# First cross attention: the spread row maxima copied to SBUF by ScalarE before the shift reads them

## The reference, cut to what matters

```python
q = _ln((x @ Wq + bq).reshape(b, s1, H, HD), qn_w, qn_b)      # 16 heads of 32
kv = jnp.concatenate([y_main @ Wk + bk, y_main @ Wv + bv], axis=-1)
k = _ln(kv[..., :HD], kn_w, kn_b)
v = kv[..., HD:]
ctx = _attn(qT, k, v)            # softmax(q k^T * scale) v, over 1585 keys
ctx_dca = _attn(qT, k_dca, v_dca)  # the last 16 keys, their own softmax
ctx = ctx + DCA_WEIGHT * ctx_dca
```

## Time and profile before

| what | value |
|---|---|
| time, median of 3 runs | 2612.16 us (2611.98 to 2613.95) |
| the profiled execution's own time | 2601.18 us |
| its span | 2599.4 us |
| PE busy | 2277.8 us (88%) |
| DVE busy | 1655.2 us (64%) |
| ACT busy | 1182.7 us (46%) |
| POOL busy | 1042.8 us (40%) |
| mean granted clock of PE | 0.944 |

### The profile page before, as it was taken

The page is one execution under the profiler, slowest core; times in us unless marked ns, Lnnn a source line. Parts: engine busy times, 40 slices in busy tenths (PEclk is TensorE's granted clock), DMA queues, the critical chain, the costliest instruction groups (busy, mean ns, idle before and its releaser), DMA issues. The chain is left out here.

```text
span 2599.4 us, 45868 instructions
## 1 busy us (share of the span) xinstructions
PE 2277.8 (88%) x16206; PEld 1809.3 (70%) x16212; DVE 1655.2 (64%) x2676; ACT 1182.7 (46%) x2172; POOL 1042.8 (40%) x724
## 2 busy tenths in 40 slices
PE   4598899989987699987997899999999998788866
PEld 2576677767765488875776688888888876566644
DVE  3457787778787333334532388878888883676763
ACT  1345555555554133322312476766677662333242
POOL 3157788878887000000110154555455560100230
PEclk9689999999997799997998999999999998899979
DMA  3000000000000211202313100000000001211200
GB/s 109 1 26 26 27 2 27 27 27 2 27 2 2 80 53 63 65 21 67 79 35 107 33 18 18 27 26 10 19 26 26 1 1 65 63 37 44 78 0 17
DMA packets 104280, 89.91 MB, mean 35 GB/s; under 512 B 32753, under 2 KB 82433, under 8 KB 104081
## 3 DMA queue, kind: packets, MB, share of 16 engines
q1 hardware_dynamic: 103792, 87.28, 11.0%
q0 software_dynamic: 288, 0.00, 0.0%
HBM read 86.22 MB, written 1.05 MB: 34 GB/s over the span
## 5 line engine op out<-in xcount | busy, mean ns | idle before, releaser
L2249 POOL TENSOR_TENSOR xT<-xT,x1b_ring 128x512 f32<-128x512 f32 (+1 forms) x176 | 249.2, 1416 | 211.8 <-ACT x1b_ring L2379 205.6
L914 POOL TENSOR_TENSOR x0b_krstd<-x0b_krstd,minus_half 128x24 f32<-128x24 f32 x64 | 269.4, 4209 | 101.8 <-DVE x0b_krstd L984 78.0
L934 POOL TENSOR_TENSOR xT<-xT,x0b_ring 128x512 f32<-128x512 f32 (+1 forms) x176 | 252.1, 1432 | 82.4 <-ACT x0b_ring L1143 72.4
L111 DVE TENSOR_TENSOR x1b_plo<-x1b_ring,x1b_phi 128x512 fp32r<-128x512 f32 (+1 forms) x208 | 221.1, 1063 | 5.2 <-issue 4.9
L1143 ACT ACTIVATE x0b_ring<-x0b_ring 128x512 f32<-128x512 f32 (+1 forms) x208 | 130.9, 631 | 188.6 <-DVE x0b_ring L1012 182.3
L2394 ACT ACTIVATE x1b_ring<-x_ps,x1b_keymask 128x512 f32<-128x512 f32 (+1 forms) x208 | 143.1, 688 | 132.9 <-DVE xT L2321 126.9
L1036 DVE TENSOR_TENSOR x0b_ring<-x_ps,x0b_krstd 128x512 f32<-128x512 f32 (+1 forms) x208 | 142.6, 686 | 76.2 <-PE x_ps L819 74.8
L116 PE MATMUL x_ps<-x1b_qy,x1b_yT 128*128 128x512 f32 (+1 forms) x416 | 175.9, 423 | 4.3 <-ACT x1b_ring L2394 2.9
L2321 DVE SCALAR_TENSOR_TENSOR xT<-x_ps,x1b_keymask,xT 128x512 f32<-128x512 f32 (+1 forms) x176 | 131.2, 746 | 58.3 <-PE x_ps L118 57.4
L116 PE MATMUL x_ps<-x1b_phi,x1b_yv 128*128 128x512 f32 (+1 forms) x416 | 165.9, 399 | 1.5 <-ACT x1b_out_sb L2361 1.5
L118 PE MATMUL x_ps<-x1b_qy,x1b_yT 128*128 128x512 f32 (+1 forms) x416 | 164.3, 395 | 0.0
(11 more groups left out here) (587 smaller groups left out, 5748.1 us busy)
## 6 DMA issues: line engine op xcount, KB each, us to landing
x_y<-in_ctx_dram SPq DMA_DIRECT2D x8, 1536.0 KB
x_y<-in_ctx_dram SPq DMA_DIRECT2D x24, 512.0 KB, 3.8
a_wn<-in_L_attn_W_Q_dram SPq DMA_DIRECT2D x16, 256.0 KB, 3.1
a_wn<-in_L_attn_W_K_dram SPq DMA_DIRECT2D x16, 256.0 KB, 3.5
a_wn<-in_L_attn_W_V_dram SPq DMA_DIRECT2D x16, 256.0 KB, 4.2
a_won<-in_L_attn_W_O_dram SPq DMA_DIRECT2D x16, 256.0 KB, 2.8
x1a_wq<-in_L_xattn_Wq_dram SPq DMA_DIRECT2D x4, 1024.0 KB, 11.5
x1c_wo<-in_L_xattn_Wo_dram SPq DMA_DIRECT2D x8, 512.0 KB, 7.3
```

The costliest lines, as they stand in the source:

```text
L111: return v.tensor_tensor(lo, exact, hi.bitcast(F32), ALU.subtract)
L914: ins = g_.tensor_tensor(r, r, c.minus_half[:, 0:8].unsqueeze(1).broadcast_to([P, whole, 8]), ALU.pow)
L934: g_.tensor_tensor(total[half][0:m, :], old, src, ALU.add).then_inc(summed, 1)
L2249: g_.tensor_tensor(total[half][0:m, :], old, src, ALU.add).then_inc(summed, 1)
```

## The change

The spread maxima lose their own bank. PE writes them into the next bank of the rotation, which now has four banks (4 to 7), ACT copies the 128 x 512 block into SBUF (into `c.xn`, of which two tiles serve as `shift`, one for each half) and gives the bank back, and all 13 shifts of the half read that copy. PE no longer waits for `shifted` before it spreads; it waits for the rotation's bank. The preparation's small product moves from bank 4 to bank 3. Nothing is removed from any engine; ACT gets 16 copies.

```diff
+        shift = [c.xn[:, f, :] for f in range(2)]
...
-        S_BANKS, O_BANK, M_BANK, KV_BANKS = (0, 1, 2), 3, 4, (5, 6, 7)
+        S_BANKS, O_BANK, KV_BANKS = (0, 1, 2), 3, (4, 5, 6, 7)
...
-                for what, at in (("sums", 29), ("inverse", 30), ("maxima", 13)):
+                for what, at in (("spread", 15), ("sums", 29), ("inverse", 30), ("maxima", 13)):
...
                     f = half_at(part, n, 15)
                     if f is not None:
+                        bank, nth = place["spread", 2 * seq + f]
+                        pe.wait_ge(kv_free[bank], nth + 1)
                         pe.wait_ge(rowmax_done, 3 * (2 * seq + f) + 3)
-                        if not (part == "first" and f == 0):
-                            pe.wait_ge(shifted, TILES * seq + KT * f)
                         for t in range(4):
-                            mm = pe.transpose(ps[:, M_BANK, t * P:(t + 1) * P],
+                            mm = pe.transpose(ps[:, bank, t * P:(t + 1) * P],
                                               rowmax[:, f % 2, t:t + 1].broadcast_to([P, P]), c.ident[:, :])
                         mm.then_inc(max_spread, 1)
+                        pe.sem_inc(kv_full[bank], 1)
...
                         if t % KT == 0:
-                            v.wait_ge(max_spread, 2 * seq + t // KT + 1)
+                            v.wait_ge(shift_kept, 2 * seq + t // KT + 1)
                         v.wait_ge(kept, TILES * seq + (t + 1))
-                        v.tensor_tensor(slot, slot, ps[0:m, M_BANK, :], ALU.subtract).then_inc(shifted, 1)
+                        v.tensor_tensor(slot, slot, shift[(t // KT) % 2][0:m, :], ALU.subtract).then_inc(shifted, 1)
...
                 def step(part, seq, n):
+                    f = half_at(part, n, 15)
+                    if f is not None:
+
+                        bank = place["spread", 2 * seq + f][0]
+                        act.wait_ge(max_spread, 2 * seq + f + 1)
+                        if 2 * seq + f >= 2:
+                            act.wait_ge(shifted, KT * (2 * seq + f - 1))
+                        act.activation(shift[f % 2], ps[:, bank, :], ACT.Copy).then_inc(shift_kept, 1)
+                        act.wait_ge(shift_kept, 2 * seq + f + 1)
+                        act.sem_inc(kv_free[bank], 1)
                     f = half_at(part, n, 30)
```

More of the change, by code:

```diff
@@ L719, in x0_main_attention @@
         out_kept, normed, added = st.sem("out_kept"), st.sem("normed"), st.sem("added")
+        shift_kept = st.sem("shift_kept")
         apart = st.sem("apart")
@@ L802, in _ @@
                     for g in range(HG0):
-                        mm = pe.matmul(ps[:, M_BANK, 16 * t + 4 * g:16 * t + 4 * g + 4], qT[:, g, t * P:(t + 1) * P],
+                        mm = pe.matmul(ps[:, O_BANK, 16 * t + 4 * g:16 * t + 4 * g + 4], qT[:, g, t * P:(t + 1) * P],
                                        headkn[:, :], start=True, stop=True)
@@ L1124, in _ @@
                     for bp in range(2):
-                        src = ps[64 * bp:64 * bp + 64, M_BANK, 0:16 * T].rearrange("p (t k a) -> p t k a", t=T, a=2)
+                        src = ps[64 * bp:64 * bp + 64, O_BANK, 0:16 * T].rearrange("p (t k a) -> p t k a", t=T, a=2)
                         dst = qshift[64 * hp:64 * hp + 64, :].rearrange("p (t a k) -> p t a k", t=T, a=2)
```

## The result

The changed kernel takes 2645.66 us (median of 4 runs, 2644.87 to 2655.12) against 2613.05 us (4 runs, 2611.98 to 2618.49): 1.0142 times the time before, 95% interval 1.0112 to 1.0172. The medians differ by 32.6 us, the ratio and its interval make it 37 (29 to 45); +5 was forecast and +24 was the upper end of the range.

A forecast was written before the change was run, and what follows sets the result against it. PE was taken to bound the kernel. Delays at four places, 9.8 + 8.4 + 3.5 + 1.6 = 23.3 us, less 18.0 of bank waits gave +5.3, so 2617.5, rounded 2618 us; range 2600 to 2636.

The forecast's parts named there:

- A: Step 0 of each sequence: late DVE work delays POOL's power and the turned sums; +1.4 us, seven times, +9.8 us.
- B: Step 14: the shift meets a POOL add, so ACT's squares come late for PE; +1.2 us, seven times, +8.4 us.
- C: Step 24: the shift meets a POOL add and ends late, ACT and PE follow; +0.5 us, seven times, +3.5 us.
- the banks: PE's waits for rotation banks: a fourth bank can remove them all, a gain of 18.0 us.
- D: End of the stage: ten shifts against POOL's last adds, some eight falling between adds at +0.2 each; +1.6 us.
- The bound: Between 200 and 780 us PE sets the pace; a gain can come only from its 51.9 idle us.
- The removed waits: Four rows of PE's bank waits can go, 18.0 us, or 20.5 with the wait for `shifted`.
- second rival: Removed waits return as data waits and stretching falls into idle time; 2612 within 5 us, chance 0.16.
- The shift's length: Unchanged alone; beside POOL's adds the shift's mean goes from 683 to 900 to 1050 ns.
- The clock is no part of it: PE's granted clock, 0.98 between 200 and 780 us, was ruled out as a factor in what bounds the kernel.
- The signs: Expected in the profile: longer shifts and adds, bank waits nearly gone, POOL waits over 3 us, squares' waits 15 or more.
- DVE becomes the bound: Late stretches on DVE join up and use its idle time, so PE waits; 2627 to 2657 us, chance 0.16.

The follow-up runs named there:

- three_banks: Changed kernel, but the spread maxima keep a bank of their own and three banks rotate; 2659.16 us, 1.0191 times the kernel before.
- small_adds_after: Changed kernel with POOL's adds cut to 8 of 512 columns; 2565.67 us, 0.9847 times the kernel before.
- small_adds_before: Kernel before with POOL's adds cut to 8 of 512 columns; 2571.43 us, 0.987 times the kernel before.
- operand: Kernel before, but all 208 shifts read an SBUF tile (wrong numbers), without copies and with three banks; 2658.38 us, ratio 1.018.
- operand_last: Kernel before, but only the last sequence's 26 shifts read SBUF (wrong numbers); 2621.94 us against 2614.07, ratio 1.0031.

## Why the forecast had the sign and not the size

The forecast's terms add up to 3.7 us by the start of the eighth sequence (A, B and C less the banks) and 1.6 from there on (D). The traces have 19.2 and 15.0. So D, the last sequence and the end, is short by 13 us, and the sequences before it by 15: of their terms A was too small, B and C did not happen as described, and the banks were counted too high.

**The bound** (PE, its idle 52 us all there is to gain): right. Of PE's waits, though, "the rest are waits for data" named two rows and passed over two more, the maxima's 8.4 us and L111's 4.2, which both grew.

**The removed waits**: right as rows (18.0 to 1.3 us), too high as time: 18.0 us were taken off, three_banks against the change gives about 13. The 1.1 us that PE waited for Y11's bank (L761) came back fully (1.3 us a sequence), of the 0.9 us of K111's bank (L116) only 0.3, and the 0.5 us that came back at step 22 are lost again at step 23 to a longer wait for L111: a bank wait that goes is in part followed by the wait for data that it hid. The prediction knew that way out (its second rival) and gave it no value in the sum.

**The shift's length**: right: 1004 ns, inside 900 to 1050, single ones up to 1.79 us, alone the same as from PSUM (689 against 684 ns). The Trainium skill (SBUF — State Buffer, section on the two separate sides) describes a lock on a port pair shared by VectorE and GpSimd, held for a whole instruction. For POOL's adds the runs agree: 1004 ns beside adds, 689 without. For POOL's power they do not, and the measurement decides: 122 DVE instructions with two SBUF inputs lie inside a running power of the changed kernel and average 689 ns.

**The places.** What a middle sequence gains or loses, in us, averaged over five of them and counted from the first scores of one tile to those of another (the first scores of a tile stand in the step before its own). The columns are kernels less the kernel before; "short adds" is small_adds_after less small_adds_before; what stands there too is not the work of POOL's adds.

| tiles, and what lies there | forecast | change | operand | short adds |
|---|---|---|---|---|
| 0 to 1, W02's squares (C) | +0.5 | 0.0 | +1.2 | 0.0 |
| 1 to 3, maxima and T02 (A) | +1.4 | +2.4 | +1.2 | 0.0 |
| 3 to 6, the turned sums | 0 | +0.4 | +0.5 | +0.5 |
| 6 to 12, K111's bank, W11 | (bank) | +0.7 | +0.8 | 0.0 |
| 15 to 18, W13 (B) | +1.2 | +0.8 | +1.7 | +0.3 |
| 18 to 19, Y11's bank | (bank) | -1.3 | 0.0 | -1.3 |
| 20 to 25 | (bank) | +0.8 | +0.1 | 0.0 |
| sum | +0.5 | +3.8 | +5.4 | -0.4 |

The forecast's sum is 3.1 for A, B and C less 2.6 for all banks.

**A, step 0, taken as +1.4 us**: place and mechanism right, size low. In the fourth sequence the maxima's wait grows by 0.72 (1.21 to 1.93), T02 leaves PE 0.42 later behind products at half the clock, and the power is 0.5 us longer (4.68, 4.17 before). It begins 0.04 us behind the start of a shift of ordinary length. These make 1.6; the remaining 0.5 lies between T02 and the turned sums, where DVE is late. The waits of L847 stayed at 2.0 us instead of going over 3, since the turned maxima ahead of them are late as well: the delay shows as a second wait (L882), not a longer first.

**B, step 14, +1.2**: this step of the prediction failed. Its shift meets no add and takes 0.68 us, in the change as in operand; POOL's add begins behind it (452.10). PE's wait for W13's squares does grow, from 0.4 to 1.0 us, but with short adds it grows to 0.9 as well: it is the old wait for `shifted`, moved. What the adds contribute is about 0.5 us, by another way (a wait of 0.4 for POOL's last sum at step 16).

**C, step 24, +0.5**: failed too in the change. Its shift takes 0.69 us and PE's wait for W02's squares stays at 0.6. With three banks, in operand and three_banks, the same shift takes 1.73 us and that wait grows to 1.6: the mechanism is real, but in the change POOL is still in its power (483.09 to 487.27 in the fourth sequence) when the shift comes, and has no add to meet it. That 0.5 us stand near this place, in the wait for L111, is a coincidence: they stand there with short adds too.

Left out: W11's squares at step 8, 0.5 to 0.7 late; the products behind the turned sums, at 1.2 GHz; and 0.8 us between steps 19 and 24.

**D, the end, +1.6**: the step of the prediction that cost most. The rate of 1.69 us for add, shift, add was right (1.67), but it was applied to the last ten adds alone. The last sequence runs in lockstep from its middle on, at 3.0 us a tile for 1.9. operand_last puts last sequence and end at 8 us (11.5 by its trace), the traces of before and after at 15. I had read step 0 as one place among 26, when it is the pattern wherever POOL has a new tile ready at each maximum.

**"The clock is no part of it"**: true of the kernel before, from which it was read, and not of the changed one: 0 to 8 us.

**The signs**: the shift's mean, the vanished bank waits and the squares' 15 us or more came as said, the last in part for another reason. The longest add, 1.78 us, says nothing, since before it was 1.74 already. L847's waits over 3 us did not come.

The time fell into the band of the rival "DVE becomes the bound" (2627 to 2657), but not by its mechanism: DVE is idle 80 of 580 us, and relieving 29 shifts at steps 0, 13, 14 and 24 gives back 18 us, 29 others 5. The copy, taken at nothing (bounds to 1 us a half), costs 5 us alone, within its interval of zero, and beside the SBUF operand hardly anything. Open are how the 18 us of bank waits divide between what is truly had and what other waits take back, and why the last sequence costs 15 us in the change and 8 to 11.5 in operand_last. The fourth bank with a shift from PSUM would want a ninth bank and wasn't tried.

In one line, by the ratios: 37 = 50 (operand and copy, of it 8 to 15 in the last sequence, 0 to 8 by the clock) less 13 (bank); forecast were 23 less 18.

## What to carry to other kernels

An operand in PSUM can be a shelter (683 ns beside POOL's adds, 1004 from SBUF): before moving it to SBUF, count for each VectorE instruction whether all its operands are then in SBUF, and find what GpSimd does beside it. Price it not by places that the timeline of before happens to show, but by the pattern (who waits when the first instruction ends), and run that pattern through every part of the loop, the drain above all, where the cover of other work is gone. A bank wait in the list is not what a bank gives (here 18 us of waits, about 13 of time); look for the wait for data that stands right behind it. And a number that comes out at a named place is no proof: near B's and C's places time is lost, but the shifts that were to cause it are not long there.

## What was not expected

- POOL's adds cost the kernel before 33 us (small_adds_before, 2571.43 against 2604.42). Without them the running maxima take 691 ns for 772, PE's waits for POOL's sum fall from 12.4 to 0.8 us, those for a T bank from 6.5 to none, and the last sequence with the end of the stage is 15 us shorter by the traces; how the 33 us divide was not tested.
- POOL's power, 128 x 24, is stretched by about 0.5 us when it begins beside a DVE instruction with two SBUF inputs (4.6 to 4.7 us for 4.17), and does not itself hold up DVE for its 4 us: shifts from SBUF inside it take 0.68 and 0.69 us (405.66 and 409.40 in the timeline above).
- PE's granted clock is 0.51 in the 3.5 us behind its wait of 1.93 us, and 1.00 in the same place with small products in the wait.
- ACT's copy of 128 x 512 from PSUM takes 598 ns, the exponential of the same shape in SBUF 631.
- A shift with both inputs in SBUF is no faster than with one in PSUM: 689 and 684 ns in the pair with short adds.
